# A cross-attention drain with shifts and value products in turn, and half of its output sent ahead on every engine

## What is computed

```python
# L0 cross-attention, 16 heads of 8, N = 8 batches, 128 queries, 128 keys
q, k, v = queries @ Wq + bq, keys @ Wk + bk, values @ Wv + bv     # queries = layernorm(x)
energy = einsum('nqhd,nkhd->nhqk', q, k) + einsum('nqhd,qkhd->nhqk', q, rel)
attn = softmax(where(mask == 0, -1e20, energy) / sqrt(8), axis=3)
out = einsum('nhqk,nkhd->nqhd', attn, v).reshape(8, 128, 128) * after_mask
x = x + out @ Wo + bo
# L0 feed-forward: its input layernorm(x) is quantised with ONE scale, from max(abs()) over all of it
```

## Time and profile before

| | |
|---|---|
| runs | 392.21, 392.24, 393.78 us; median 392.24 us |
| the profiled execution | 392.62 us, of which the span from first to last instruction is 390.8 us |
| PE, DVE, ACT, POOL busy | 340.4 us (87%), 320.9 us (82%), 273.4 us (70%), 66.6 us (17%) |
| TensorE clock granted, mean | 0.989 of full |

### The profile page before, as it was taken

The page is one execution under the profiler, slowest core; times in us unless marked ns, Lnnn a source line. Parts: engine busy times, 40 slices in busy tenths (PEclk is TensorE's granted clock), DMA queues, the critical chain, the costliest instruction groups (busy, mean ns, idle before and its releaser), DMA issues.

```text
span 390.8 us, 10135 instructions
## 1 busy us (share of the span) xinstructions
PE 340.4 (87%) x3970; PEld 243.3 (62%) x3970; DVE 320.9 (82%) x717; ACT 273.4 (70%) x702; POOL 66.6 (17%) x53
## 2 busy tenths in 40 slices
PE   2899998998867879997798889899999999997676
PEld 0388897896533435554456656576677767666565
DVE  4989979953779999979599999999898998986353
ACT  1678775664455257776656888998989898986673
POOL 2000020002044040000222223220232323122110
PEclk9999999999998999999999999999999999999899
DMA  8914574340000000000000000000000000000001
GB/s 313 383 33 77 67 108 69 58 71 17 0 0 1 3 0 2 2 2 0 2 2 2 0 2 0 3 2 0 3 0 2 1 3 2 1 2 3 0 0 55
DMA packets 19183, 12.56 MB, mean 32 GB/s; under 512 B 17600, under 2 KB 17856, under 8 KB 18880
## 3 DMA queue, kind: packets, MB, share of 16 engines
q1 hardware_dynamic: 19136, 11.91, 12.6%
HBM read 7.19 MB, written 0.52 MB: 20 GB/s over the span
## 4 chain that ended last, share of the span: by engine, by line
PE 43%; DVE 27%; ACT 16%; issue 11%; DMA 2%; DVEq 0%; ACTq 0%
PE ps L267 12%; PE ps L583 4%; PE ps L521 3%; DVE blk L1193 3%; DVE ss_floor L1203 3%; ACT PT L1536 3%; PE ps L442 2%; ACT PT L1606 2%; PE ps L508 2%; PE ps L627 2%; DVE Y L887 2%; PE ps L715 2%; PE ps L597 2%; PE ps L637 2%; DVE lneg L1219 2%
## 5 line engine op out<-in xcount | busy, mean ns | idle before, releaser
L1742 POOL TENSOR_TENSOR blk<-blk 128x1024 f32<-128x1024 f32 x16 | 37.8, 2361 | 168.2 <-DVE blk L1197 123.2
L583 PE MATMUL ps<-w_f,full 128*128 128x512 f32 x96 | 47.3, 609 | 0.9 <-issue 0.9
L1536 ACT ACTIVATE PT<-ps,lneg 128x128 f32<-128x128 f32 x128 | 45.2, 378 | 3.9 <-DVE lneg L1219 3.8
L1426 ACT ACTIVATE St<-ps 128x512 bf16<-128x512 f32 x32 | 19.1, 596 | 19.6 <-PE ps L267 19.6
L267 PEld LDWEIGHTS ps<-blk,st 128*128 128x128 bf16 x768 | 26.8, 98 | 3.8
L1536 ACT ACTIVATION_READ_ACCUMULATOR PT<-ps,lneg 128x1 f32 x128 | 27.9, 218 | 0.0
L267 PE MATMUL ps<-blk,rel 128*128 128x64 bf16 x768 | 27.6, 193 | 0.0
L267 PE MATMUL ps<-blk,st 128*128 128x64 bf16 x768 | 27.6, 193 | 0.0
L1593 ACT ACTIVATE PT<-ps 128x512 f32<-128x512 f32 x32 | 17.4, 594 | 12.9 <-PE ps L521 12.9
L930 DVE TENSOR_TENSOR blk<-blk,keep_b 128x1024 bf16<-128x1024 bf16 x32 | 21.9, 687 | 5.1 <-ACT blk L1413 5.0
L1061 DVE TENSOR_REDUCE mneg<-OT 128x4 bf16<-128x512 bf16 x32 | 21.5, 678 | 4.9 <-DMA OT<-St 4.4
(11 more groups left out here) (233 smaller groups left out, 836.5 us busy)
## 6 DMA issues: line engine op xcount, KB each, us to landing
w_f<-f_dram SPq DMA_DIRECT2D x2, 1689.0 KB, 13.5
w_x<-l_dram SPq DMA_DIRECT2D x1, 774.0 KB, 6.0
w_f<-ffn_dram SPq DMA_DIRECT2D x1, 561.0 KB, 8.2
X<-x_dram SPq DMA_DIRECT2D x1, 512.0 KB, 3.7
ctxT<-ctxT_dram SPq DMA_DIRECT2D x1, 512.0 KB, 4.5
OT<-maskT_dram SPq DMA_DIRECT2D x1, 512.0 KB, 7.3
OT<-St SPq DMA_TRANSPOSE x32, 2.6
const<-const_dram SPq DMA_DIRECT2D x1, 388.0 KB, 6.5
```

What stands on the lines that cost most here:

```text
L583: m = mm(ps[:, c, :], hT[:, n, :], w_f[:, l, F_QKV + 512 * c:F_QKV + 512 * (c + 1)], start=True, stop=True)
L1536: e = a(S1[:, i % 2, P * k:P * (k + 1)], ps[:, 3 + c, P * j:P * (j + 1)], ACT.Exp, bias=lneg[:, i % 2, k:k + 1], accum_out=lsum[:, i % 2, ...
L1742: g_.tensor_tensor(R[:, i % 2, :], R[:, i % 2, :], T2, ALU.add).then_inc(sem("pair_sum"), 1)
```

## The change

1. `mneg` has four slots instead of two; the reduction of chunk k waits for shift k - 4 instead of k - 2.
2. The last chunk, 31, is no longer turned by DMA: PE transposes its bf16 copy into a free PSUM bank (`turn_last_chunk`), and DVE reduces from there.
3. In the drain PE alternates: shift 28, values 4, turn of chunk 31, shift 29, values 5, shift 30, values 6, shift 31, values 7. `turn_outputs_back(0, 1)` moves from ahead of shift 31 to behind group 1's first value product; ACT's `take_outputs(0, 1)` moves behind the last exponential.
4. Group 1's first half is transposed after value product 4 instead of 5, `turn_first_o(0)` comes before product 7 instead of after it, `project_first_o(0)` before `turn_outputs_back(1, 1)`. ACT does `take_output(0, 0)` before `take_outputs(1, 1)`, and DVE moves `divide(1, 1)` from before `add_projection(0, 0)` to between `moments(1, ...)` and `normalise(1, ...)`.

```diff
@@ -137,7 +137,7 @@
         rest = sb("rest", [T])
         St = sb("St", [2, 512])
         PT = sb("PT", [HG * NB * P])
-        mneg = sb("mneg", [2, 4], BF16)
+        mneg = sb("mneg", [4, 4], BF16)
         O = sb("O", [NB, P])
         OT = sb("OT", [NB, P])
         high_b = O[:, 0:4, :].rearrange("p n q -> p (n q)").bitcast(BF16)
@@ -228,6 +228,8 @@
             src = (part, part1)[g][:, :, :].rearrange("p b (n t o) -> p (b n) t o", n=NB, o=1)
             return src[:, :, q:q + QC, :].to_broadcast([P, 2 * NB, QC, 2])
 
+        last_turned = ps[:, (G * NCH) % BANKS, 0:256].bitcast(BF16)
+
         block = stack.enter_context(nc.Block())
 
 
@@ -242,7 +244,7 @@
             sp.dma_start(w_f[:, 0, :], f_d[0]).then_inc(sem("f_in"), 16)
             sp.dma_start(w_f[:, 1, :], f_d[1]).then_inc(sem("f_in"), 16)
 
-            for c in range(G * NCH):
+            for c in range(G * NCH - 1):
                 if c == NCH:
                     sp.wait_ge(sem("st_set"), 3)
                     sp.dma_start(w_x1, l1_d).then_inc(sem("l1_in"), 16)
@@ -361,11 +363,19 @@
                         last = add(bank[:, :, i, :], rl[:, g, off:off + P], ring[:, c % RING, b, :, i, :])
                 last.then_inc(sem("scores"), 1)
 
+            def turn_last_chunk(c):
+
+                pe.wait_ge(sem("st_copied"), c + 1)
+                pe.wait_ge(sem("expd"), c - 4)
+                for j in range(4):
+                    i = tr(last_turned[:, P * j:P * (j + 1)], St_b[:, c % 4, P * j:P * (j + 1)], ident_b[:, :])
+                i.then_inc(sem("last_turned"), 1)
+
             def shift_chunk(c):
                 pe.wait_ge(sem("chunk_max"), c + 1)
                 for j in range(4):
                     i = add(ps[:, c % BANKS, P * j:P * (j + 1)],
-                            mneg[:, c % 2, j:j + 1].to_broadcast([P, P]), negid_b[:, :])
+                            mneg[:, c % 4, j:j + 1].to_broadcast([P, P]), negid_b[:, :])
                 i.then_inc(sem("shifted"), 1)
 
 
@@ -393,11 +403,8 @@
 
             pe.wait_ge(sem("consts_b"), 1)
             pe.wait_ge(sem("penalties"), 1)
-            for c in range(G * NCH + LAG):
-                if c < G * NCH:
-                    score_chunk(c)
-                if c == G * NCH + LAG - 1:
-                    turn_outputs_back(0, 1)
+            for c in range(G * NCH):
+                score_chunk(c)
                 if c >= LAG:
                     shift_chunk(c - LAG)
 
@@ -405,16 +412,21 @@
                     weigh_values(0, c - 21)
                 if c == 26:
                     turn_outputs_back(0, 0)
-                if G * NCH <= c < G * NCH + 2:
-                    weigh_values(0, 2 * (c - G * NCH) + 4)
-                    weigh_values(0, 2 * (c - G * NCH) + 5)
+            for k in range(LAG):
+                shift_chunk(G * NCH - LAG + k)
+                weigh_values(0, 4 + k)
+                if k == 0:
+                    turn_last_chunk(G * NCH - 1)
             for n in range(NB):
                 weigh_values(1, n)
-                if n == 5:
+                if n == 0:
+                    turn_outputs_back(0, 1)
+                if n == 4:
                     turn_outputs_back(1, 0)
-            turn_first_o(0)
+                if n == 6:
+                    turn_first_o(0)
+            project_first_o(0)
             turn_outputs_back(1, 1)
-            project_first_o(0)
 
 
 
@@ -1055,10 +1067,15 @@
                     set_ring(c + RING - 1)
                 if c >= LAG - 1:
                     k = c - LAG + 1
-                    dve.wait_ge(sem(f"chunk_back{k % 4}"), 16 * (k // 4 + 1))
-                    if k >= 2:
-                        dve.wait_ge(sem("shifted"), k - 1)
-                    v.tensor_reduce(mneg[:, k % 2, :], turned_b[:, k % 4, :, :], AX.X, ALU.max).then_inc(sem("chunk_max"), 1)
+                    if k < G * NCH - 1:
+                        dve.wait_ge(sem(f"chunk_back{k % 4}"), 16 * (k // 4 + 1))
+                        turned = turned_b[:, k % 4, :, :]
+                    else:
+                        dve.wait_ge(sem("last_turned"), 1)
+                        turned = last_turned.rearrange("p (j k) -> p j k", j=4)
+                    if k >= 4:
+                        dve.wait_ge(sem("shifted"), k - 3)
+                    v.tensor_reduce(mneg[:, k % 4, :], turned, AX.X, ALU.max).then_inc(sem("chunk_max"), 1)
                 if c == 27:
                     divide(0, 0)
                 if c in (2, 3, 4):
@@ -1076,9 +1093,9 @@
                     quantise_weight((18, 19, 20, 21, 22, 24, 25).index(c))
             divide(0, 1)
             divide(1, 0)
-            divide(1, 1)
             add_projection(0, 0)
             moments(1, X, 0, 4)
+            divide(1, 1)
             normalise(1, X, Y, "y", 0, 4)
             add_projection(0, 1)
             moments(2, X, 4, NB)
@@ -1441,11 +1458,12 @@
                     act.wait_ge(sem("shifted"), c + 1)
                     a(PA[c // NCH][:, :, :, q:q + QC], ps[:, c % BANKS, :].rearrange("p (n q h) -> p h n q", q=QC, n=NB),
                       ACT.Exp, scale=SOFT).then_inc(sem("expd"), 1)
-                if i in (25, 33):
-                    take_outputs(0, (i - 25) // 8)
+                if i == 25:
+                    take_outputs(0, 0)
+            take_outputs(0, 1)
             take_outputs(1, 0)
+            take_output(0, 0)
             take_outputs(1, 1)
-            take_output(0, 0)
             act.wait_ge(sem("wqT_ps"), 1)
             for m in range(2):
                 a(wqT[:, m, :], ps[:, 4, 192 * m:192 * m + I0 // 2].bitcast(BF16), ACT.Copy).then_inc(sem("wqT"), 1)
```

## The result

| | before | changed |
|---|---|---|
| median of 16 runs each | 392.94 us | 396.23 us |
| ratio, 95% interval | | 1.0075 (1.0057 to 1.0093) |
| profiled execution, its span | 392.62, 390.8 us | 396.66, 394.6 us |
| TensorE clock granted, mean | 0.989 | 0.987 |

The change made the kernel slower: by 2.9 us going by the ratio on record, by 3.3 going by the two medians. The forecast was 394.7 with 393.3 to 396.0, made against a median of 392.24. The kernel before came out 0.7 higher when both were measured here; the ratio on 392.24 gives 395.2, inside the range, while the changed kernel's own median of 396.23 stands just above its end.

The account below looks back on a forecast made before the run. No engine alone was the bound, only the chain through the stage (PE 43% of it). Terms: -0.34 + 2.47 = +2.13 us with the clock held, +2.6 where it falls; forecast 394.7 us, range 393.3 to 396.0.

Parts of the forecast that it names:

- The drain: End of the chunk loop: reordered shifts and PE's turn of chunk 31 start group 1's value products 0.98 us earlier.
- What was left at the first addition: First half's addition after its Wo product: 0.34 us of gain remains, inserted transposes and a moved copy taking 0.64.
- The division behind the moments: DVE, ACT and PE between moments and normalise: the moved division makes this stretch 2.47 us longer.
- PE's queue: PE work behind the second half's Wo product, from 103.76 us: later, but no cost at full clock.
- The clock: TensorE's clock halves after PE's sparse stretch in more executions than not, delaying the spread about 0.45 us.
- the gap: PE's sparse stretch from about 100.3 to 103.8 us, holding one group of transposes, 0.66 us busy in 3.5.
- rival 5: Clock falls twice or low stretches shift onto the chain, up to 1.7 us each; 395.5 to 396.5, chance 0.08.
- the rows did not keep their distances: After the spread of the maximum: the forecast said the rows should keep their distances.
- a sign of being wrong: After the spread of the maximum: the forecast is wrong if that stage gives time back.
- The front gain: From drain to first addition: the whole 0.98 us comes through, sum +1.5, time 393.7; chance 0.13.
- The loop before the drain: Chunk loop before 86 us: four mneg slots bring back about 2.1 us, time 392.2; chance 0.06.

Follow-up runs that it names:

- e3: The change's drain alone, with the output order of the kernel before on PE, ACT and DVE; ratio 0.9984 against the kernel before.
- e7: The change's drain, reordered, with the output order of before and some transposes of group 1 moved; 393.01 against 393.55 us for the kernel before, ratio 0.9985.
- e1: The changed kernel with ACT's root of the first half ahead of the copy take_output(0, 1); 395.56 against 393.97 us for the kernel before, ratio 1.0059.
- e2: The changed kernel with DVE's divide(1, 1) between the first addition and the moments; ratio 1.0020 against the kernel before.
- e4: The kernel before with only the change's output order on PE, ACT and DVE; 395.68 against 393.97 us, ratio 1.0082.
- e5: The changed kernel measured once more, unaltered; 395.51 us, ratio 1.0052 against the kernel before.
- e6: The changed kernel with ten more unread products on PE where it waits before the second half's Wo product; 394.88 us, ratio 1.0034 against the kernel before.

## Why the prediction was right

*The drain* gave 0.88 of the 0.98 forecast (0.81 with the offset of chunk 29 out). Four transposes of chunk 31 took 0.40, 0.22 each and overlapped, as the 0.3 to 0.4 worked out from the weights' transposes. The Trainium skill's figure of some 275 ns for one in a kernel (TensorE: Matmul & The Clock Gate, Part 4: PE-mode transpose), an estimated 1.1 for four in a row, was not met. The reduction from PSUM, bounded from 0.64 to twice that, took 0.68 as from SBUF.

*What was left at the first addition*: 0.17 in the profile as it stands (0.10 with the offset out), where I had 0.34; the term was mis-sized by the 0.10 of the drain and another 0.07 on the way to `turn_first_o(0)`, and its sign and cause were right. e3 shows that the drain by itself gains nothing there. That the inserted transposes and the wait ahead of them take it is read from the rows, not tested alone; e7, which places them one product later among other moves, gains 0.37 there with the offset out.

*The division behind the moments* was the forecast's main term, 2.47 from the end of the moments to `normalise`. From 101.39 to 104.19 less the 0.58 of before it is 2.22: the division began 0.08 before the last of the moments ended, and the root 0.11 before the copy ahead of it did, where I had put each behind the other. The sum at the spread is 2.05 (2.12 with the offset out) against 2.13, and that it is so close is partly luck: 0.25 too much loss here and 0.17 too much gain above cancel. e1 shows that ACT's order makes the wait ahead of `normalise`, e2 that DVE's own time is 0.9 to 1.1 of the price and the place behind the moments the rest, e4 that it comes without the drain.

*PE's queue* cost nothing at full clock, as forecast: the second half's transposes started at 109.77, 0.18 later than 107.54 and the 2.05, and PE still waited 0.62 for DVE's maximum ahead of the spread.

*The clock* fell in the gap in two of the four traces with this gap left open (e4 and e5; not in the first trace of the changed kernel and not in e1), where I had said more executions than not. It cost 0.58 in e5 (0.45 forecast) and 1.7 in e4, where it stayed down for 6.8 us and not for the 3.4 of the forecast.

The first profiled execution of the changed kernel had this term at nothing in the gap and lost its 1.8 beyond the edit at 194 us and at the end: that is rival 5's mechanism, to which I gave 0.08, and its 396.66 lies above that rival's 396.5. From the spread on the rows did not keep their distances, as I had said they would, and near 123 us the kernel gave 0.4 back, which I had named as a sign of being wrong; e3's trace, without the division moved, does the same (0.02 behind at 115, 0.41 ahead at 133), because the fall of before at 123 is missing in it. So the mechanism up to the spread is shown, and the last 0.8 us of the 2.9 are the clock's as far as the rows and the averages of e5 and e6 go, in places that I had not forecast.

The Trainium skill (TensorE: Matmul & The Clock Gate, Part 1: The HAM clock gate) has the half clock for an idle array and the full one for sustained work. The rows of e4 and e5 agree in direction, though PE was not idle in the gap but busy 1.22 and 1.14 of 4 us: the clock fell there, and it came back behind a busy stretch, at 110 and at 108.5. With the same gap it held in the changed kernel's first trace and in e1.

*The rivals.* The front gain did not come through whole (e3). The loop before the drain did not get shorter by more than 0.15: ACT copied the last chunk at 86.46 against 86.61, and the changed kernel was as far ahead at 11 us (11.20 against 11.36), before the first chunk. The two measured ratios of the changed kernel, 1.0075 and 1.0052, are 2.9 and 2.0 us; the forecast's 2.13 to 2.6 lies between.

## What to carry to other kernels

Price a moved instruction by who stands behind what it releases, on every engine, and not by its own duration: a division of 1.1 us cost 2.2, its own time, since its engine no longer waited there, and as much again because another engine's queue held the next step behind its consumer. Taking one such order back may not bring its wait back: in e1 it brought 0.7, since the next thread ended shortly before. Work that stands in an engine's wait is free, and out of it it is not; ask of each step where the wait is that hides it before moving it. A wait also has a second price on TensorE, since a sparse stretch can bring the half clock to the dense one behind it, as in e4 and e5.

## What was not expected of the hardware

When the clock falls is not the same from one execution to the next: of two traces of the same program, one has it at half at 105 to 108.5 and 125.5 to 129 us, the other not until 194, although PE was busy 1.14 and 1.13 of the 4 us from 100 to 104. In e4 it stayed at half for 6.8 us (103.2 to 110) although PE was busy 5.91 of the 6 us from 104 on, and so it did in the changed kernel's first trace near the end (371.4 to 378, PE busy 5.90 of the 6 from 372 on); the falls in the gap of e5 and at 123 before lasted some 3.4. I have no run that says why. The reduction of a bf16 bank took 681 ns from PSUM and 679 from SBUF (median of 31).
